# An attention and feed-forward block on one NeuronCore: three projection jobs of the second batch moved in halves behind the first row maxima

## The chip, the cores and the metric

The kernel runs on 1 core of one Trainium2 chip. The metric is the device time in microseconds (us) of one execution; lower is better. The kernel before took 443.47 us, the median of 3 runs (442.30 to 444.01).

## What is computed

Two batches of 1024 tokens with 128 features pass through 16-head attention (8 features a head), a residual with a layer norm, a feed-forward part of gated and GELU layers with 512 hidden features, and a second residual with a layer norm. Cut to what matters here:

```python
q, k, v = proj(wq, bq), proj(wk, bk), proj(wv, bv)   # x @ w.T + b, split into 16 heads
scores = einsum('bhqd,bhkd->bhqk', q, k) / sqrt(16)
out = einsum('bhqk,bhkd->bhqd', softmax(scores, axis=-1), v)
x = layernorm(x + out @ wo.T + bo)
x = layernorm(x + ffn(x))
```

The softmax takes the maximum of each row of scores before the exponential, so the kernel computes all scores twice: once for the maxima alone, and once, with the keys on the partitions, for the exponential.

## The kernel before, in words

**Work units.** The attention is cut into 16 units, each of 4 heads and 512 query rows of one batch. For each unit the maxima of its rows are found by 16 *turns*; a turn computes the scores of one head and 128 query rows against all 1024 keys (two matmuls of 512 columns), and the vector engine (DVE) reduces them to one maximum a row. The maxima of a unit are split into three bfloat16 parts by GpSimd (POOL, `split_max`), turned by TensorE (PE, `turn_max`), copied out of PSUM by ScalarE (ACT, `copy_max`) and written by two DMAs of the SyncE queue (SP, `load_max`, L466 and L406) into extra rows of the query tile `qx`, so that the second pass subtracts the maximum inside its matmul.

**The order of the work.** There is no scheduler: every engine has its own program written out in order, and waits on semaphores. PE's program at the start is: nine fill matmuls, the four projection jobs of the first batch (`job(0)` to `job(3)`, L1234), two matmuls that give the difference of the keys of the two halves (L1256, L1257), the v projection (L1263), then projection jobs of the second batch, then the first maxima. A projection job is one chunk of 512 tokens times the weights of q or k (`JOBS`, L188: of the second batch k of chunk 2, k of chunk 3, q of chunk 2, q of chunk 3, which are jobs 4 to 7). `AHEAD_JOBS` (L190) says how many of the eight jobs run whole before the first maxima; a later one runs as two `half_job`s of 256 columns (L1237), one behind each turn.

**The first maxima.** The first 27 turns (`WHOLE`) go without scores beside them. The first five (`FOLD`) are *unfolded*: two matmuls by `turn_half` (L1291) and one reduction over 1024 columns on DVE (`turn`, L958). Turns 5 to 26 are *folded*: `fold_apart` (L1319) computes the scores against the difference of the key halves, ACT copies its positive part out of PSUM (`copy_over`, L685), `fold_first` (L1307) computes the scores of the first half, and DVE adds both and reduces 512 columns instead of 1024 (`turn_folded`, L967). `busy` (L1223) issues fill matmuls whose result nobody reads. Turn 0 waits for the first rows of k and q, which SP and ACT load back from DRAM (`rows_first`, L1287), and for the four v chunks that DVE takes out of the same banks (`v_ready`, L1376).

**The evacuation of the jobs.** For each job of the second batch ACT copies the PSUM bank out with the bias (L655, which counts `proj_ready`), and makes the rounded copy (L658); POOL subtracts the two (L846), and SP stores the results to DRAM (L508, L512), where the units of the second batch load them. ACT's program has the four jobs (L653) ahead of its first `copy_over` (L687). PE waits for `proj_ready` to reach 4 (L1390) ahead of the first `fold_apart`.

**Behind it.** After turn 26 the main part begins: groups of three turn halves, three score matmuls (L1353, with `exp` on ACT, L664) and value products (L1369).

```python
JOBS = [("k", 0), ("k", 1), ("q", 0), ("q", 1), ("k", 2), ("k", 3), ("q", 2), ("q", 3)]
EARLY = 4
for t in range(FOLD):
    turn_half(2 * t)
    turn_half(2 * t + 1)
```

Of the kernel before, what the change touches and what calls it, by code (L numbers as in the profile page):

```python
# [42 lines left out]
C = 512  # L43
# [143 lines left out]

JOBS = [("k", 0), ("k", 1), ("q", 0), ("q", 1), ("k", 2), ("k", 3), ("q", 2), ("q", 3)]  # L188
EARLY = 4
WARM, OLD_FILL_BANK, FILL_BANK, AHEAD_JOBS = 9, 0, 7, 6  # L190


def gate_bank(c, m):
# [19 lines left out]
def build(nc, xT, wqT, wkT, wvT, woT, bq, bk, bv, bo, late,  # L213
          w1s, w2s, h1s, h2s, w3s, k_dram, q_dram, d_dram, den_dram, out):
    with ExitStack() as ctx:
# [3 lines left out]
        def sem(name):  # L219
            return ctx.enter_context(nc.semaphore(name))  # L220
# [43 lines left out]
        attn_c = xT_sb  # L264

        den_c = [sb(f"den_c{n}", [P, (u1 - u0) * C * HG // P]) for n, (_, u0, u1) in enumerate(MOVES)]
        v_sb = sb("v_sb", [P, G_ALL, KT, HG * DH])
        v_pad = sb("v_pad", [P, 2, KT, HG, 32])
# [45 lines left out]
        split_low = sem("split_low")  # L314
# [7 lines left out]
        proj_ready = sem("proj_ready")  # L322
# [896 lines left out]
        def _(pe):  # L1219
            def busy(n, bank, cols=C):  # L1220

                for _ in range(n):
                    nc.tensor.matmul(ps[:, bank, 0:cols], nonzero[:, 0, 0:P], nonzero[:, 0, 0:cols],  # L1223
                                     start=True, stop=True)
# [12 lines left out]
            def half_job(n, j):  # L1237

                name, c = JOBS[n]
                at = slice(j * C // 2, (j + 1) * C // 2)  # L1240
                ins = nc.tensor.matmul(ps[:, JOB_BANKS[n % 4], at], (wq_sb if name == "q" else wk_sb)[:],
                                       xT_sb[:, c * C + j * C // 2:c * C + (j + 1) * C // 2], start=True, stop=True)
                if j == 1:
                    ins.then_inc(job_done, 1)
# [25 lines left out]
            def turn_half(m):  # L1270

                t, part = m // 2, m % 2
                slot, qc, (h, q) = t // (QC * TURNS) % 2, t // TURNS % QC, head_of(t)
                at, h = slice(h // PAIR * GROUP, h // PAIR * GROUP + TROWS), h % PAIR
                if 2 * WHOLE <= m < 2 * WHOLE + 4:

                    pe.wait_ge(max_taken, 2 * (m - WHOLE - 3))
                elif m >= 4:

                    pe.wait_ge(max_taken, m - 3)  # L1280
                if part == 1 and t % (QC * TURNS) == 0 and t >= PER * TURNS:

                    pe.wait_ge(rows_late[slot], t // (PER * TURNS) * LOAD_INC[1])
                if part == 0:
                    if t == 0:

                        pe.wait_ge(rows_first, LOAD_INC[0])  # L1287
                    elif t % TURNS == 0:

                        pe.wait_ge(rows_in[slot][qc], (t // (PER * TURNS) + 1) * LOAD_INC[qc])  # L1290
                nc.tensor.matmul(ps[:, half_bank(m), :],  # L1291
                                       qx[at, slot, qc, h, q * P:(q + 1) * P],
                                       kx[at, slot, h, part * C:(part + 1) * C], start=True, stop=True)\
                  .then_inc(max_scores, 1)
# [84 lines left out]
            for t in range(FOLD):  # L1379
                turn_half(2 * t)  # L1380
                turn_half(2 * t + 1)
                if t < 2 * (len(JOBS) - AHEAD_JOBS):
                    half_job(AHEAD_JOBS + t // 2, t % 2)
                else:
                    pe.wait_ge(proj_ready, 1)
                    busy(1, OLD_FILL_BANK)
                    busy(1, OLD_FILL_BANK, C // 2)
            pe.wait_ge(kd_set, 2)
            pe.wait_ge(kd_in, LOAD_INC[1])
            pe.wait_ge(proj_ready, EARLY)  # L1390
# [259 lines left out]
```

## Time and profile before

| | |
|---|---|
| time, median of 3 runs | 443.47 us (442.30 to 444.01) |
| profiled execution, first to last instruction (span) | 441.5 us |
| that execution's own time | not listed beside the runs; the median lies 1.97 us above its span |
| PE busy | 427.8 us (97%) |
| DVE busy | 386.5 us (88%) |
| ACT busy | 367.7 us (83%) |
| POOL busy | 90.3 us (20%) |

A profile's row of a timeline has the start and the length in us, the engine, the line of the kernel, the operation, what it writes and reads, the number of instructions merged into the row, and in brackets how long the engine sat idle before it and what released it. `PEld` is PE's load of weights, `SPq` the queue of SyncE. A float32 matmul against the full weights stands as two instructions in the trace. Some matmul records are missing from a trace.

### The profile page before, as it was taken

The page shows a single profiled execution, that of the slowest core. Times are in us where ns is not written, and L with a number is a line of the kernel's source. Part 1 is how long each engine was busy: PE and PEld are TensorE (multiplying, and loading weights), DVE is VectorE, ACT ScalarE, POOL GpSimd, SP SyncE. Part 2 cuts the span into 40 slices and gives each one's busy share as a digit, 9 for nine tenths or more (in the row PEclk, how much of TensorE's full clock was granted, in tenths as well). Part 3 has the DMA queues.
Part 4 walks back from the last instruction along what each step waited for, and adds up shares of the span by engine and source line. Part 5 has one row for each costly group of instructions (what it writes and reads, how often), then busy time and mean ns, then how long its engine had stood idle before and what let it go on. Part 6 is the DMA issues. An engine that isn't in the chain of part 4 may idle for free.

```text
span 441.5 us, 9824 instructions
## 1 busy us (share of the span) xinstructions
PE 427.8 (97%) x3496; PEld 227.0 (51%) x3498; DVE 386.5 (88%) x719; ACT 367.7 (83%) x694; POOL 90.3 (20%) x142
## 2 busy tenths in 40 slices
PE   8999999999999999999999999999899899999995
PEld 4543544444444444444444443544333488877884
DVE  6799999999999999999999999999884577657636
ACT  4487989998998999989899899999899886678762
POOL 9730000100000010000001002373311263046103
PEclk9999999999999999999999999999999999999999
DMA  6567741111130110113011001021021000000101
GB/s 165 176 196 129 270 147 33 44 28 28 48 122 25 45 31 28 27 48 122 25 46 33 26 27 49 14 43 47 15 39 50 13 8 1 1 2 2 48 1 48
DMA packets 17117, 24.88 MB, mean 56 GB/s; under 512 B 5169, under 2 KB 9009, under 8 KB 16689
## 3 DMA queue, kind: packets, MB, share of 16 engines
q1 hardware_dynamic: 16464, 23.68, 19.3%
q10 hardware_dynamic: 608, 0.59, 0.5%
q8 instruction: 30, 0.49, 0.5%
q14 instruction: 15, 0.11, 0.1%
HBM read 15.08 MB, written 7.60 MB: 51 GB/s over the span
## 4 chain that ended last, share of the span: by engine, by line
PE 76%; DVE 10%; ACT 5%; SPq 3%; DMA 2%; issue 2%; POOL 0%; POOLq 0%; DVEq 0%; ACTq 0%
PE ps L1369 24%; PE ps L1291 20%; PE ps L1479 16%; DVE negmax L977 9%; PE ps L1353 8%; ACT arena L664 2%; DMA parts_q<-arena 2%; PE ps L1223 2%; PE ps L1234 1%; PE ps L1423 1%; PE ps L1319 1%; PE ps L1263 1%; SPq L463 1%; SPq L435 1%; ACT v_pad L722 1%
## 5 line engine op out<-in xcount | busy, mean ns | idle before, releaser
L977 DVE TENSOR_REDUCE negmax<-ps 128x1 f32<-128x512 f32 x458 | 275.8, 701 | 1.8 <-PE ps L1291 1.5
L664 ACT ACTIVATE arena<-ps 128x512 f32<-128x512 f32 x360 | 190.0, 606 | 19.3 <-PE ps L1353 14.1
L1353 PE MATMUL ps<-qx,kx 64*128 64x512 f32 x512 | 171.3, 451 | 0.9 <-DMA qx<-mT 0.6
L1291 PE MATMUL ps<-kx,qx 61*128 61x512 f32 x468 | 160.2, 441 | 0.6 <-DMA qx<-parts_q 0.5
L1291 PEld LDWEIGHTS ps<-kx,qx 61*128 61x128 f32 x468 | 75.1, 184 | 88.6 <-DVE negmax L977 79.3
L1369 PE MATMUL ps<-arena,v_pad 128*32 128x256 f32 (+3 forms) x1328 | 104.8, 407 | 2.8 <-ACT arena L664 2.8
L664 ACT ACTIVATE hf<-ps 128x512 f32<-128x512 f32 x152 | 83.2, 604 | 9.4 <-PE ps L1353 8.4
L1353 PEld LDWEIGHTS ps<-qx,kx 64*128 64x128 f32 x512 | 78.9, 184 | 18.6 <-ACT arena L664 11.8
L1479 PE MATMUL ps<-hid,w_high 128*128 128x512 f32 (+1 forms) x296 | 68.3, 388 | 0.8 <-issue 0.4
L1479 PEld LDWEIGHTS ps<-hid,w_high 128*128 128x128 f32 x296 | 54.2, 188 | 12.3 <-issue 0.8
L1369 PEld LDWEIGHTS ps<-arena,v_pad 128*32 128x32 f32 x1328 | 28.5, 108 | 37.1 <-issue 30.7
L1369 PE MATMUL ps<-hf,v_pad 128*32 128x128 f32 (+1 forms) x600 | 47.5, 388 | 0.0
L1120 DVE TENSOR_TENSOR hid<-hf,hid 128x512 fp32r<-128x512 f32 x32 | 23.0, 727 | 19.6 <-ACT hid L738 19.6
L829 POOL TENSOR_TENSOR mpart<-negmin,zeros 128x16 bf16<-128x16 f32 x15 | 3.3, 220 | 145.5 <-DVE negmin L987 145.5
L888 POOL TENSOR_TENSOR hid<-hf,hid 128x512 fp32r<-128x512 f32 x16 | 20.6, 1317 | 32.6 <-ACT hid L728 32.6
L1369 PEld LDWEIGHTS ps<-hf,v_pad 128*32 128x32 f32 x600 | 15.7, 109 | 16.1 <-issue 9.9
L809 POOL COPY v_pad<-v_sb 128x256 f32 (+1 forms) x8 | 3.1, 398 | 87.2 <-PE ps L1369 87.1
L737 ACT ACTIVATE hf<-ps,h2s_sb 128x512 f32<-128x512 f32 x16 | 11.0, 688 | 10.7 <-PE ps L1479 10.7
L737 ACT ACTIVATE hf<-ps,h1s_sb 128x512 f32<-128x512 f32 x16 | 11.0, 686 | 8.7 <-PE ps L1479 8.7
L1102 DVE SCALAR_TENSOR_TENSOR hf<-ps,w2s_sb,v_pad 128x512 f32<-128x512 f32 x16 | 11.5, 740 | 7.3 <-ACT v_pad L722 7.3
L857 POOL TENSOR_TENSOR w_low<-late_sb,w_high 128x512 fp32r<-128x512 f32 x11 | 14.1, 1282 | 16.4 <-ACT w_high L711 16.4
L1479 PE MATMUL ps<-prt,w_high 128*128 128x512 f32 x64 | 16.4, 403 | 0.6 <-DVE hf L1102 0.6
(107 smaller groups left out, 317.2 us busy)
## 6 DMA issues: line engine op xcount, KB each, us to landing
qx<-parts_q SPq DMA_DIRECT2D x60, 64.0 KB, 2.1
late_sb<-in_late SPq DMA_DIRECT2D x3, 1280.0 KB, 5.5
kx<-parts_k SPq DMA_DIRECT2D x56, 64.0 KB, 2.2
parts_q<-prt SPq DMA_DIRECT2D x3, 512.0 KB, 6.4
parts_q<-arena SPq DMA_DIRECT2D x3, 512.0 KB, 8.3
xT_sb<-in_xT SPq DMA_DIRECT2D x4, 256.0 KB, 4.2
xT_sb<-arena SPq DMA_DIRECT2D x28, 32.0 KB
prt<-den SPq DMA_DIRECT2D x7, 128.0 KB
```

The lines of the kernel that those rows point to most:

```text
L664: nc.scalar.activation(probs(n // HG)[:, heads(n), :], ps[:, PLAN["score", n][0], :], ACT.Exp, scale=SCALE).then_inc(exp_done, 1)
L737: nc.scalar.activation(hf[:, m % RING, :], bank, ACT.Gelu, scale=scale).then_inc(gelu_done, 1)
L857: nc.gpsimd.tensor_tensor(half(w_low[:, n, :]), w_sb[:, n, :], w_high[:, n, :], ALU.subtract).then_inc(w_left, 1)
L888: nc.gpsimd.tensor_tensor(half(dst[:, 1, m, :]), hf[:, m % RING, :], dst[:, 0, m, :], ALU.subtract).then_inc(gate_ready, 1)
L977: nc.vector.tensor_reduce(negmax[:, t // TURNS % 2, m % 2, h * QT + q:h * QT + q + 1], ps[:, MAX_BANK + m % 4, :], AX.X, ALU.max, negate=T ...
L1102: return nc.vector.scalar_tensor_tensor(out=out, in0=ps[:, gate_bank(c, m) + 1, :], scalar=s_sb["w2s"][:, m:m + 1], in1=gate[:, m % 2, :], ...
L1120: nc.vector.tensor_tensor(half(dst[:, 1, m, :]), hf[:, m % RING, :], dst[:, 0, m, :], ALU.subtract).then_inc(gelu_ready, 1)
L1223: nc.tensor.matmul(ps[:, bank, 0:cols], nonzero[:, 0, 0:P], nonzero[:, 0, 0:cols], start=True, stop=True)
L1291: nc.tensor.matmul(ps[:, half_bank(m), :], qx[at, slot, qc, h, q * P:(q + 1) * P], kx[at, slot, h, part * C:(part + 1) * C], start=True, s ...
L1353: nc.tensor.matmul(ps[:, bank, :], kx[at, slot, h % PAIR, kt * P:(kt + 1) * P], qx[at, slot, qc, h % PAIR, :], start=True, stop=True)\
L1369: ins = nc.tensor.matmul(ps[32 * n:32 * n + 32, PLAN["pv", w][0], c0:c1], v_pad[:, w // QC % 2, kt, n, :], probs(k)[:, n, c0:c1], start=(k ...
L1479: return nc.tensor.matmul(dsts[n], half(stationary), half(moving), start=start, stop=stop)
```

## The change

`AHEAD_JOBS` goes from 6 to 5. Job 5 (k of chunk 3) no longer runs whole ahead of turn 0. Jobs 5, 6 and 7 run as six halves: one behind each of the five unfolded turns, and the sixth, the second half of job 7, directly behind the fifth. The wait for `proj_ready` and the two fill matmuls behind turn 4 go away, and `half_job` gains the wait for the bank (`split_low`) that `job` has.

```diff
-WARM, OLD_FILL_BANK, FILL_BANK, AHEAD_JOBS = 9, 0, 7, 6
+WARM, FILL_BANK, AHEAD_JOBS = 9, 7, 5
...
             def half_job(n, j):
 
                 name, c = JOBS[n]
+                if j == 0:
+                    pe.wait_ge(split_low, n - EARLY + 1)
...
             for t in range(FOLD):
                 turn_half(2 * t)
                 turn_half(2 * t + 1)
-                if t < 2 * (len(JOBS) - AHEAD_JOBS):
-                    half_job(AHEAD_JOBS + t // 2, t % 2)
-                else:
-                    pe.wait_ge(proj_ready, 1)
-                    busy(1, OLD_FILL_BANK)
-                    busy(1, OLD_FILL_BANK, C // 2)
+                half_job(AHEAD_JOBS + t // 2, t % 2)
+            half_job(len(JOBS) - 1, 1)
             pe.wait_ge(kd_set, 2)
             pe.wait_ge(kd_in, LOAD_INC[1])
             pe.wait_ge(proj_ready, EARLY)
```

The lines below L1237 move down by two or up by two; ACT, DVE and SP have the same instructions in the same order, and POOL too. PE's order changes at two places. At the first, between the v projection and turn 1, PE has before (L1234 a whole job, L1291 the two halves of a turn, L1241 a half job):

```order
L1263 MATMUL ps<-wv_sb,xT_sb 128x128 x16
L1234 MATMUL ps<-xT_sb,wk_sb 128x512 x2
L1291 MATMUL ps<-kx,qx 128x512 x2
L1241 MATMUL ps<-xT_sb,wq_sb 128x256
L1291 MATMUL ps<-kx,qx 128x512 x2
```

and now (L1265, L1293 and L1243 are the same lines, shifted):

```order
L1265 MATMUL ps<-wv_sb,xT_sb 128x128 x16
L1234 MATMUL ps<-xT_sb,wk_sb 128x512
L1293 MATMUL ps<-kx,qx 128x512 x2
L1243 MATMUL ps<-xT_sb,wk_sb 128x256
L1293 MATMUL ps<-kx,qx 128x512 x2
```

One whole job less stands ahead of turn 0, and the half behind turn 0 is now one of the moved k job. At the second place, from turn 3 to the first folded pair (L1319, L1307), PE has before:

```order
L1291 MATMUL ps<-kx,qx 128x512 x2
L1241 MATMUL ps<-xT_sb,wq_sb 128x256
L1291 MATMUL ps<-kx,qx 128x512 x2
L1223 MATMUL ps<-hf 128x512
L1223 MATMUL ps<-hf 128x256
L1319 MATMUL ps<-w_high,qx 128x512 x2
L1307 MATMUL ps<-kx,qx 128x512 x2
```

and now:

```order
L1293 MATMUL ps<-kx,qx 128x512 x2
L1243 MATMUL ps<-xT_sb,wq_sb 128x256
L1293 MATMUL ps<-kx,qx 128x512 x2
L1243 MATMUL ps<-xT_sb,wq_sb 128x256 x2
L1321 MATMUL ps<-w_high,qx 128x512 x2
L1309 MATMUL ps<-kx,qx 128x512 x2
```

The two fills behind turn 4 have given way to the two halves of job 7, of which the last stood ahead of turn 4 before.

## Rows read from the trace of the kernel before

**Rows 1.** The page: span, busy time of each engine, granted clock by slice.
```profile
span 441.5 us, 9824 instructions
...
PE 427.8 (97%) x3496; PEld 227.0 (51%) x3498; DVE 386.5 (88%) x719; ACT 367.7 (83%) x694; POOL 90.3 (20%) x142
...
PEclk9999999999999999999999999999999999999999
```

**Rows 2.** Chain that ended last, in order: start us, us, what.
```profile
13.84 1.72 PE ps L1234 x4
15.56 0.66 PE ps L1291 x2
16.22 0.63 PE ps L1241 x2
...
20.76 0.70 ACT late_sb L655
...
32.90 0.29 ACT mT L672
33.21 0.92 SPq L406
```

**Rows 3.** Windows: span; PE, PEld, DVE, ACT, POOL busy; PEclk; DMA share; GB/s.
```profile
56.40:200.00 143.60, 142.82 (x1444) 66.46 (x1446) 143.00 (x246) 129.19 (x254) 8.44 (x36) 1.00 0.16 49
```

**Rows 4.** Timeline of PE, 15 to 28 us.
```profile
15.49 0.73 PE L1291 MATMUL ps<-kx,qx 61*128 61x512 f32 x2
...
20.02 0.70 PE L1241 MATMUL ps<-xT_sb,wq_sb 128*128 128x256 f32 x2
20.65 0.73 PE L1291 MATMUL ps<-kx,qx 61*128 61x512 f32 x2
21.54 0.27 PE L1223 MATMUL ps<-hf 128*128 128x256 bf16 x1 [0.16 <-ACT late_sb L655]
21.74 0.50 PE L1319 MATMUL ps<-w_high,qx 61*128 61x512 f32 x2
...
27.68 0.85 PE L1319 MATMUL ps<-w_high,qx 61*128 61x512 f32 x2
```

**Rows 5.** Timeline of ACT, 20 to 33 us.
```profile
20.76 0.69 ACT L655 ACTIVATE late_sb<-ps,bq_sb 128x512 f32<-128x512 f32 x1 [1.23 <-PE ps L1241]
21.48 0.63 ACT L658 ACTIVATE prt<-late_sb 128x512 fp32r<-128x512 f32 x1
22.28 2.18 ACT L685 ACTIVATE arena<-ps 128x512 f32<-128x512 f32 x4 [0.17 <-PE ps L1319]
...
29.66 3.35 ACT L685 ACTIVATE arena<-ps 128x512 f32<-128x512 f32 x6 [0.37 <-PE ps L1319]
```

**Rows 6.** Timeline of DVE, 13 to 37 us.
```profile
13.88 0.69 DVE L946 TENSOR_TENSOR v_sb<-ps,bv_bc 128x512 f32<-128x512 f32 x1 [0.20 <-PE ps L1263]
...
16.33 6.37 DVE L958 TENSOR_REDUCE negmax<-ps 128x1 f32<-128x1024 f32 x5 [1.72 <-PE ps L1291]
23.01 0.69 DVE L967 CUSTOM_DVE_ANT_0 arena<-ps,arena 128x512 f32<-128x512 f32 x1 [0.30 <-ACT arena L685]
...
36.65 0.69 DVE L977 TENSOR_REDUCE negmax<-ps 128x1 f32<-128x512 f32 x1
```

**Rows 7.** SP's last two loads for turn 0: lengths in ns, starts, landing.
```profile
L400 SPq DMA_DIRECT2D qx<-parts_q x2: 418/419/420, 12.2 to 12.6; - x2
...
DMA to landing us min/median/max: 2.1/2.2/2.2
```

**Rows 8.** Timeline of ACT, the last four copies of the folded turns.
```profile
33.19 2.27 ACT L685 ACTIVATE arena<-ps 128x512 f32<-128x512 f32 x4
```

**Rows 9.** Timeline of PE, the fills that wait for these copies.
```profile
35.60 0.59 PE L1223 MATMUL ps<-hf 128*128 128x512 bf16 x2 [0.48 <-ACT arena L685]
```

**Rows 10.** Timeline of POOL, the first step of splitting unit 0's maxima.
```profile
29.97 0.22 POOL L829 TENSOR_TENSOR mpart<-negmax,zeros 128x16 bf16<-128x16 f32 x1 [4.65 <-DVE negmax L967]
```

**Rows 11.** SP's waits, 14 to 60 us: total us, times, longest.
```profile
SPq L406 <- ACT mT L672: 3.4, 1, 3.4
```

**Rows 12.** Timeline of PE at the wait for unit 1's maxima.
```profile
56.37 0.47 PE L1353 MATMUL ps<-qx,kx 64*128 64x512 f32 x1 [0.58 <-DMA qx<-mT]
```

**Rows 13.** PE's waits, whole span: total us, times, longest.
```profile
PE ps L1369 <- ACT arena L664: 2.8, 5, 0.9
```

## The prediction, made before the changed kernel was run

> **What bounds the kernel now.** I read four views, from the whole to the place of the change. The page [rows 1] comes first: PE is busy for 97% of the span, DVE for 88%, ACT for 83%, and the clock row stands at 9 tenths or more in all slices, so no time is lost to TensorE's lower clock. Shares over the whole span do not say what a start-up change is worth; two other views do. The chain that ended last [rows 2] runs in the start-up through PE without a gap (two whole jobs, then turn, half job, turn, half job), at 20.76 through ACT's evacuation of job 7, later through ACT's copy of the first maxima at 32.90 and at 33.21 into SP's queue. The windows [rows 3] show what follows: from 56.4 to 200 us DVE is busy for 143.0 of 143.6 us and PE for 142.8. There is nothing there to catch up with, so whatever moves the instant at which the main part starts should move the end by about as much.
>
> The timelines then show who waits for whom at the change. On PE [rows 4] turn 0 begins at 15.49 the moment the whole jobs let go, the second half of job 7 runs from 20.02 to 20.72, turn 4 follows, and the first folded pair starts at 21.74. On ACT [rows 5] the evacuation of job 7 begins at 20.76, its rounded copy ends at 22.11 (21.48 + 0.63), and the first copy of a folded turn begins at 22.28, released by PE. On DVE [rows 6] the five unfolded turns go from 16.33 to 22.70, DVE waits 0.30 us for ACT's first copy, starts the first folded turn at 23.01 and then has 22 of them without a gap worth naming until 36.65, 0.62 us each. So the start of the folded turns on DVE is set by ACT, and ACT stands behind the last projection job.
>
> **The change, part by part.**
>
> *Turn 0 earlier.* One whole job (half of 1.72 us, 0.86 [rows 2]) leaves the place ahead of turn 0. Job 4 now ends at 13.84 + 0.86 = 14.70. Turn 0 has two other conditions. DVE's fourth v chunk ends at 14.57 (13.88 + 0.69 [rows 6]). Its rows are loaded by SP: the last issue starts at 12.6 and lands 2.1 to 2.2 us later [rows 7], so at 14.7 to 14.8. From the release to a matmul I take 0.14 us: ACT's last folded copy ends at 33.19 + 2.27 = 35.46 [rows 8], and PE's fills that wait for it start at 35.60 [rows 9]. Turn 0 then starts at 14.94 instead of 15.49, 0.55 us earlier: not the whole 0.86, since the load is late next.
>
> *Six half jobs for four.* A turn takes PE 0.66 us and a half job 0.63 [rows 2]. Split in halves, job 5 costs 1.26 us instead of 0.86, with a weight load exposed at each half. From turn 0 to the end of job 7 PE now has 5 turns and 6 halves, 3.30 + 3.78 = 7.08 us. The last two halves stand side by side with the same weights; in the whole jobs a matmul record of 512 columns takes 1.72 / 4 = 0.43 us, so a half with hidden weights would take 0.43 in two records, and the last half may be up to 0.20 cheaper. I take 6.98. Job 7 ends at 14.94 + 6.98 = 21.92, against 20.72 before: **1.20 us later**, though everything started 0.55 earlier. It ended ahead of turn 4 before; now turn 4 and one half more stand before it.
>
> *What waits for job 7.* ACT starts its evacuation 0.04 us after the end (20.72 to 20.76), at 21.96; it takes 0.69, to 22.65. PE needs it for `proj_ready` at 4, so the first folded pair starts at 22.65 + 0.14 = 22.79 against 21.74, 1.05 later. ACT's own order gives the same: evacuation and rounded copy take 1.35 us (20.76 to 22.11), to 23.31, and the first folded copy needs PE's pair, which came 0.54 us ahead of it before (21.74 to 22.28), so it starts at 23.33 against 22.28. DVE's first folded turn then moves from 23.01 to 24.06, **1.05 us later**, though DVE is through with the unfolded ones about 0.55 us earlier: it waits for ACT for some 1.9 us instead of 0.30.
>
> *The fills and the waits.* The two fills behind turn 4 lie in a time in which PE waits for ACT now anyway: nothing. The added waits for `split_low` ask for splits that DVE has done before the v chunk of 13.88 [rows 6], since DVE works in order: nothing. POOL gets job 7's copies 1.2 us later, but sat idle for 4.65 us ahead of the maxima at 29.97 [rows 10]: hidden. SP stores the results of these jobs behind the maxima in its own order, which is later still: hidden.
>
> *What may give some back.* At turn 16 the pair on PE took 0.85 us instead of 0.50 (27.68 against 21.74 [rows 4]), because the query rows of unit 1 had just landed, and ACT lost 0.37 us behind it [rows 5]. The load does not move, so this wait vanishes once the turns come a microsecond later. DVE had no gap there, so on DVE's side nothing is gained; if ACT's copies are what decides, the delay shrinks by 0.37.
>
> *To the end.* DVE's folded turns, the copy of the maxima at 32.90 and SP's write at 33.21 [rows 2] follow one after the other. SP had waited 3.4 us for that copy [rows 11], so its queue moves by the same amount, and it is SP's queue that PE waits for again at 56.37 [rows 12]. From there DVE and PE are full [rows 3].
>
> The sum is +1.05 us on the profiled span, 441.5 to 442.5. That execution's own time is not listed; the median of the runs, 443.47, lies 1.97 above its span, and I carry that over: **444.5 us**. The bounds of the terms are +0.58 (the last half as cheap as it can be, which is 0.10 less, and the 0.37 given back) and +1.15 (no saving on the last half). I stay near the upper end because DVE, not ACT, goes without a gap through the folded turns.
>
> **A rule against this change.** The change leaves PE idle for about 0.9 us between job 7 and the first folded pair, where fills stood. The trace has a wait of that length elsewhere, 0.9 us of PE on ACT [rows 13], and the clock row shows no slice below 9 tenths [rows 1]. The Trainium skill (TensorE: Matmul & The Clock Gate, section "A second HAM failure mode: psum-queue depth-cycling") says that short idle stretches between groups of matmuls, when frequent, can let TensorE fall to its lower clock and back. By that rule the time would come out as in the third rival below; by the rows it costs nothing.
>
> **The rivals.**
>
> *The earlier start carries through.* If the folded turns could begin as soon as DVE is free, the 0.55 us of turn 0 would be the gain: 443.47 - 0.55 = 442.9 us. For it: turn 0 does start earlier, and DVE stood idle for 1.72 us ahead of it [rows 6]. Against it: ACT's copy, which DVE waited for already [rows 6], is behind job 7's evacuation in ACT's own order. It needs halves that cost PE far less than 0.63 us. Chance 0.12.
>
> *Swallowed.* The delay ends in waits that stood there before: the 0.37 on ACT [rows 5] and the 0.58 us at 56.37 [rows 12], for instance if SP's queue there were held by landings that do not move. Then 1.05 - 0.37 - 0.58 = 0.1, or 443.6 us. Against it: SP's wait of 3.4 us [rows 11] says that its queue starts with the maxima. Chance 0.13.
>
> *The clock falls: slower.* If PE's clock goes to the lower of its two levels (1.2 and 2.4 GHz) in the idle 0.9 us, a round of the fold loop, which now takes two of DVE's folded turns, 1.24 us, would be set by PE: its work in a round lies near 1.15 us (0.50 for the pair [rows 4], 0.59 for two fills [rows 9], something for `fold_first`), and doubled it is 2.3, about 1.1 us more a round. One round already makes +2.15 in all, three make 444.5 + 3.3 = 447.8 us, all eleven 456.6. It decides from the first round on. Chance 0.05.
>
> That the change does not do what it says is excluded by the order of the instructions.
>
> **How the numbers follow.** The forecast, 444.5 us with its own range 444.0 to 445.1, has 0.66; the rivals 0.12, 0.13 and 0.05; 0.04 is left for a slower time of another kind. The runs before spread from 442.30 to 444.01, so a median of a few runs can be off by half a microsecond. The range reaches down to the first rival and up to the upper bound with that scatter: 442.8 to 445.7. A measurement of this kernel tells about 0.5%, 2.2 us, from no change: the forecast, +0.2%, and the first two rivals lie within, so 0.88 for the same, 0.03 for faster (a quarter of the first rival, by scatter) and 0.09 for slower (the clock and the rest).
>
> **What would show it.** In the profile after, PE's turn 0 starts near 14.9, the last half job ends near 21.9, the first folded pair starts near 22.8 with about 0.9 us idle ahead of it released by ACT L655; ACT's first L685 row starts near 23.3, DVE's first folded row near 24.1, ACT's copy of the maxima near 33.9. The forecast is wrong if DVE's first folded turn comes before 23.0, if that delay is gone again by SP's L406, or if PE's clock row dips.

## The result and the profile after

The changed kernel takes **443.84 us**, the median of 20 runs (443.32 to 445.98), against 443.04 us for the kernel before in 20 runs of the same comparison (442.20 to 444.01). The ratio is 1.0023, with a 95% interval of 1.0015 to 1.0031: about 1.0 us slower (0.0023 x 443). The medians lie 0.80 us apart; three of the 20 executions of the changed kernel took over 445 us, and they weigh more in the ratio than in the median. The prediction had +1.05 us and 444.5 us.

The page of the kernel after, for [rows 1]: span, busy time, granted clock by slice.

```profile
span 442.9 us, 9825 instructions
...
PE 428.8 (97%) x3498; PEld 228.0 (51%) x3498; DVE 386.4 (87%) x719; ACT 368.4 (83%) x694; POOL 90.5 (20%) x142
...
PEclk9999999999999999999999999999999999999998
```

The engines have as much to do as before, and the clock row has no dip in the start-up. Its 8 stands in the last of 40 slices, at the end of the span. What differs has to be looked for in waits. The timeline of PE after, for [rows 4]:

```profile
14.53 1.02 PE L1234 MATMUL ps<-xT_sb,wk_sb 128*128 128x512 f32 x2
16.03 0.69 PE L1293 MATMUL ps<-kx,qx 61*128 61x512 f32 x2 [0.48 <-DMA qx<-parts_q]
...
21.81 1.13 PE L1243 MATMUL ps<-xT_sb,wq_sb 128*128 128x256 f32 x4
23.81 0.49 PE L1321 MATMUL ps<-w_high,qx 61*128 61x512 f32 x2 [0.87 <-ACT late_sb L655]
...
29.72 0.52 PE L1321 MATMUL ps<-w_high,qx 61*128 61x512 f32 x2
```

Turn 0 is now released by the landing of its rows, and no longer by the jobs. The two halves of job 7 stand side by side and end at 22.94 (21.81 + 1.13). PE then stands idle for 0.87 us until ACT's evacuation has counted `proj_ready`. The timelines of ACT and of DVE after, for [rows 5] and [rows 6]:

```profile
22.98 0.69 ACT L655 ACTIVATE late_sb<-ps,bq_sb 128x512 f32<-128x512 f32 x1 [0.37 <-PE ps L1243]
23.70 0.63 ACT L658 ACTIVATE prt<-late_sb 128x512 fp32r<-128x512 f32 x1
24.31 10.70 ACT L685 ACTIVATE arena<-ps 128x512 f32<-128x512 f32 x18
34.90 0.29 ACT L672 ACTIVATE mT<-ps 128x128 f32<-128x128 bf16 x1
```

```profile
16.84 6.38 DVE L958 TENSOR_REDUCE negmax<-ps 128x1 f32<-128x1024 f32 x5 [1.38 <-PE ps L1293]
25.05 0.69 DVE L967 CUSTOM_DVE_ANT_0 arena<-ps,arena 128x512 f32<-128x512 f32 x1 [1.84 <-ACT arena L685]
...
38.66 0.69 DVE L977 TENSOR_REDUCE negmax<-ps 128x1 f32<-128x512 f32 x1
```

ACT's first folded copy begins the moment the rounded copy of job 7 ends, and DVE, which waited 0.30 us for that copy before, waits 1.84.

The whole start-up of this profiled execution lies later than before, which is not the change's doing: its first fills and jobs, the same instructions in the same order as before, ran slower. Two rows of each timeline of PE, before and then after:

```profile
1.25 3.62 PE L1223 MATMUL ps<-hf 128*128 128x512 bf16 x9 [1.25 <-DVE hf L933]
...
4.86 1.98 PE L1234 MATMUL ps<-xT_sb,wk_sb 128*128 128x512 f32 x4
```

```profile
1.26 4.02 PE L1223 MATMUL ps<-hf 128*128 128x512 bf16 x9 [1.26 <-DVE hf L933]
...
5.07 2.62 PE L1234 MATMUL ps<-xT_sb,wk_sb 128*128 128x512 f32 x4
```

What slowed them no view says; the clock row shows nothing here in either profile. So I compare stretches. Job 4 is the first job of the second batch; its first matmul starts at 13.68 before and at 14.53 after. In the 13 profiles of this document it starts from 13.47 to 14.89 where job 5 stands whole ahead of turn 0, and from 13.89 to 14.53 where it does not, so this start varies from execution to execution. The stretch from there to DVE's first folded turn is called the lead-in below.

| stretch, us | before | after | difference |
|---|---|---|---|
| start to job 4's first matmul | 13.68 | 14.53 | +0.85 |
| job 4 to turn 0 | 1.81 | 1.50 | -0.31 |
| turn 0 to the end of job 7 | 5.23 | 6.91 | +1.68 |
| turn 0 to DVE's first folded turn | 7.52 | 9.02 | +1.50 |
| **lead-in: job 4 to DVE's first folded turn** | 9.33 | 10.52 | **+1.19** |
| first folded turn to the main part (DVE's first L977) | 13.64 | 13.61 | -0.03 |
| main part to the end of the span | 404.85 | 404.24 | -0.61 |

The lead-in took 1.19 us more, and all of it was still there where the main part starts. The -0.61 behind it is looked at last.

### The profile page after: what moved, and what is told of

Same layout as the page of the kernel before. It is cut to its first block, busy times and chain, and to the rows that moved or that the text cites. A ratio compares the mean times of both kernels' runs of the same rounds, so it can differ in the third digit from the quotient of the medians.

```text
span 442.9 us, 9825 instructions
## 1 busy us (share of the span) xinstructions
PE 428.8 (97%) x3498; PEld 228.0 (51%) x3498; DVE 386.4 (87%) x719; ACT 368.4 (83%) x694; POOL 90.5 (20%) x142
## 4 chain that ended last, share of the span: by engine, by line
PE 78%; DVE 11%; ACT 5%; issue 2%; DMA 1%; POOL 0%; SPq 0%; POOLq 0%; DVEq 0%; ACTq 0%
PE ps L1371 25%; PE ps L1293 21%; PE ps L1477 15%; DVE negmax L977 9%; PE ps L1355 9%; ACT arena L664 2%; PE ps L1223 2%; PE ps L1421 1%; PE ps L1321 1%; PE ps L1243 1%; PE ps L1309 1%; ACT v_pad L722 1%; DMA qx<-parts_q 1%; PE ps L1431 0%; DVE hf L1102 0%
## 5 line engine op out<-in xcount | busy, mean ns | idle before, releaser
L977 DVE TENSOR_REDUCE negmax<-ps 128x1 f32<-128x512 f32 x458 | 275.8, 724 | 1.2 <-PE ps L1293 0.9
L664 ACT ACTIVATE arena<-ps 128x512 f32<-128x512 f32 x360 | 190.3, 607 | 19.0 <-PE ps L1355 13.4
L1293 PE MATMUL ps<-kx,qx 61*128 61x512 f32 x468 | 160.0, 441 | 0.8 <-DMA qx<-parts_q 0.5
L1293 PEld LDWEIGHTS ps<-kx,qx 61*128 61x128 f32 x468 | 75.0, 184 | 88.4 <-DVE negmax L977 78.6
L664 ACT ACTIVATE hf<-ps 128x512 f32<-128x512 f32 x152 | 83.4, 605 | 8.6 <-PE ps L1355 7.2
```

The source lines that it names most:

```text
L664: nc.scalar.activation(probs(n // HG)[:, heads(n), :], ps[:, PLAN["score", n][0], :], ACT.Exp, scale=SCALE).then_inc(exp_done, 1)
L977: nc.vector.tensor_reduce(negmax[:, t // TURNS % 2, m % 2, h * QT + q:h * QT + q + 1], ps[:, MAX_BANK + m % 4, :], AX.X, ALU.max, negate=T ...
L1293: nc.tensor.matmul(ps[:, half_bank(m), :], qx[at, slot, qc, h, q * P:(q + 1) * P], kx[at, slot, h, part * C:(part + 1) * C], start=True, s ...
```

## The experiments

The theory: the time follows the lead-in, which is set by the end of the last moved job, through ACT's order and PE's wait for `proj_ready` alike. The rivals: one of the two waits alone decides; the removed fills matter; the time comes from elsewhere in the program. Each ratio is taken against executions of the kernel before that ran beside the kernel named; their medians lie between 442.94 and 443.37 us, so two rows are compared by their ratios and not by their medians. In all diffs the line numbers shift by a few.

| kernel | job 4 to turn 0, us | turn 0 to first folded turn, us | lead-in | median of runs, us | ratio to before (95%) |
|---|---|---|---|---|---|
| before | 1.81 | 7.52 | 9.33 | 443.04 | 1 |
| the change | 1.50 | 9.02 | 10.52 | 443.84 | 1.0023 (1.0015 to 1.0031) |
| e3_job7_ahead | 1.26 | 8.54 | 9.80 | 443.38 | 1.0006 (0.9996 to 1.0017) |
| e5_pe_not_waiting | 1.37 | 8.93 | 10.30 | 443.83 | 1.0019 (1.0010 to 1.0028) |
| e7_act_alone | 1.18 | 9.02 | 10.20 | 443.90 | 1.0025 (1.0013 to 1.0036) |
| e6_both | 1.20 | 8.27 | 9.47 | 443.53 | 1.0012 (1.0002 to 1.0022) |
| e2_fills_back | 1.32 | 9.03 | 10.35 | 443.56 | 1.0014 (1.0002 to 1.0027) |
| e1_last_half_behind | 1.81 | 8.46 | 10.27 | 443.23 | 1.0015 (0.9998 to 1.0032) |
| e10_last_half_again | 1.81 | 8.16 | 9.97 | 444.84 | 1.0031 (1.0013 to 1.0049) |
| e8_last_half_and_fills | 1.81 | 8.16 | 9.97 | 444.23 | 1.0022 (1.0012 to 1.0032) |
| e11_fills_again | 1.81 | 8.16 | 9.97 | 443.44 | 1.0008 (0.9996 to 1.0020) |
| e4_whole_job6 | 1.81 | 6.87 | 8.68 | 442.40 | 0.9991 (0.9978 to 1.0003) |
| e9_whole_job6_again | 1.82 | 6.87 | 8.69 | 442.61 | 0.9987 (0.9975 to 0.9998) |

The lead-in of `e1_last_half_behind` holds 0.30 us more than that of the same kernel in `e10_last_half_again`, because its profile was already under the lower clock at the first folded pair, as shown below.

### Job 7's end moved back ahead of the fifth turn

From the changed kernel, with both halves of job 7 behind turn 3:

```diff
-                half_job(AHEAD_JOBS + t // 2, t % 2)
-            half_job(len(JOBS) - 1, 1)
+                if t < FOLD - 1:
+                    half_job(AHEAD_JOBS + t // 2, t % 2)
+                if t == FOLD - 2:
+                    half_job(len(JOBS) - 1, 0)
+                    half_job(len(JOBS) - 1, 1)
```

> The changed kernel with both halves of job 7 moved ahead of turn 4, so that turn 4 covers their evacuation. Theory: job 7 ends about 0.6 us earlier against turn 0, D near 9.9, ratio to before about 1.001, 0.5 us below the changed kernel. Rival (the number of halves or the place of job 5 decides): D near 10.5, ratio 1.002.

The timeline of PE in this kernel:

```profile
15.39 0.70 PE L1293 MATMUL ps<-kx,qx 61*128 61x512 f32 x2 [0.23 <-DMA qx<-parts_q]
...
19.89 1.56 PE L1243 MATMUL ps<-xT_sb,wq_sb 128*128 128x256 f32 x6
21.38 0.73 PE L1293 MATMUL ps<-kx,qx 61*128 61x512 f32 x2
22.70 0.50 PE L1321 MATMUL ps<-w_high,qx 61*128 61x512 f32 x2 [0.59 <-ACT late_sb L655]
```

Three half jobs in a row take 1.56 us, and turn 4 now covers part of ACT's evacuation. Turn 0 to the first folded turn shrinks from 9.02 to 8.54, and the time with it, from +1.0 to +0.3 us (0.0006 x 443). The order of the halves alone, with the same work, moves the lead-in as the end of job 7 does. The time moves the same way, but its interval (-0.2 to +0.8 us) holds zero and overlaps that of the change.

### PE's wait, ACT's order, and both

`e5_pe_not_waiting` lets PE start the first folded pair after three evacuations, and asks for the fourth ahead of the first fill of the fold loop. In `e7_act_alone` PE waits as in the change, but ACT makes the rounded copy of job 7 only behind the first four folded copies. `e6_both` has both edits.

```diff
-            pe.wait_ge(proj_ready, EARLY)
+            pe.wait_ge(proj_ready, EARLY - 1)
             for t in range(FOLD, WHOLE, 2):
...
+                if t == FOLD:
+                    pe.wait_ge(proj_ready, EARLY)
                 busy(1, FILL_BANK)
```

```diff
                   .then_inc(proj_ready, 1)
-                act.wait_ge(proj_ready, n + 1)
...
+                if n < EARLY - 1:
+                    round_job(n)
...
                 copy_over(t)
+                if t == FOLD + 3:
+                    round_job(EARLY - 1)
```

> The changed kernel, but PE waits for three evacuated jobs ahead of the first folded pair (its banks are those of jobs 4 to 6) and for the fourth only ahead of the first fill, which writes job 7's bank. Let F be the time from turn 0's first matmul to DVE's first folded turn: 7.52 us before, 9.02 after. Theory: ACT's own order (evacuation and rounded copy of job 7 ahead of the first folded copy) holds the folded turns as well, so PE's pair comes 0.9 us earlier, F stays 8.9 to 9.0, and the time is that of the changed kernel (ratio 1.002). Rival (PE's wait alone holds them): F near 8.2, ratio 1.000 to 1.001.

> The changed kernel with the rounded copy of job 7 on ACT put behind the first four folded copies; PE waits as in the changed kernel. Theory: PE's pair now holds the folded turns alone, F stays near 9.0, and the copy costs DVE a gap of about 0.4 us at the fifth folded turn: time of the changed kernel or 0.3 us more (ratio 1.002 to 1.003). Rival (ACT's order alone holds them): F near 8.4, ratio 1.001.

> Both edits, the shorter wait on PE and the later rounded copy on ACT. Theory: only with both gone do the folded turns start sooner, F near 8.4 (job 7's evacuation of 0.7 us still stands ahead of them on ACT); some 0.4 of the 0.6 us is given back at the fifth folded turn, where ACT now makes the copy: ratio 1.001 to 1.002. Rival (neither holds them, the end of turn 4 does): F near 9.0.

The timeline of ACT without PE's wait, `e5_pe_not_waiting`:

```profile
22.21 0.69 ACT L655 ACTIVATE late_sb<-ps,bq_sb 128x512 f32<-128x512 f32 x1 [0.37 <-PE ps L1243]
22.93 0.63 ACT L658 ACTIVATE prt<-late_sb 128x512 fp32r<-128x512 f32 x1
23.47 2.04 ACT L685 ACTIVATE arena<-ps 128x512 f32<-128x512 f32 x4
```

PE's pair stands there at 22.10, ahead of ACT's evacuation, and still ACT's first folded copy comes behind the rounded copy: turn 0 to the first folded turn is 8.93, not shorter than 9.02 by anything that counts. The timeline of ACT with ACT's order alone changed, `e7_act_alone`:

```profile
22.20 0.69 ACT L662 ACTIVATE late_sb<-ps,bq_sb 128x512 f32<-128x512 f32 x1 [0.37 <-PE ps L1251]
23.53 2.22 ACT L691 ACTIVATE arena<-ps 128x512 f32<-128x512 f32 x4 [0.65 <-PE ps L1329]
25.63 0.63 ACT L657 ACTIVATE prt<-late_sb 128x512 fp32r<-128x512 f32 x1
```

Now ACT is free at 22.89 and waits 0.65 us for PE's pair: 9.02 again. Only with both edits does the copy follow the evacuation at once, in the timeline of ACT of `e6_both`:

```profile
22.49 0.69 ACT L662 ACTIVATE late_sb<-ps,bq_sb 128x512 f32<-128x512 f32 x1 [0.37 <-PE ps L1251]
23.07 2.21 ACT L691 ACTIVATE arena<-ps 128x512 f32<-128x512 f32 x4
```

The stretch falls to 8.27 and the time to +0.5 us. The lead-in of 9.47 is 0.14 above before, and the moved copy leaves DVE a gap of 0.17 us ahead of its fifth folded turn; together that is 0.3 us, within the interval (0.1 to 1.0 us). So each of the two waits is enough to hold the folded turns, and neither alone is the cause.

### The fills

To the changed kernel, behind the last half of job 7, the two fills come back (into bank 0):

```diff
             half_job(len(JOBS) - 1, 1)
+            pe.wait_ge(proj_ready, 1)
+            busy(1, 0)
+            busy(1, 0, C // 2)
```

> The changed kernel with the two fill matmuls put back, behind the last half of job 7. Theory: they run inside PE's idle 0.87 us, so D stays near 10.5 and the time is that of the changed kernel (ratio 1.002 to before). Rival (the missing fills cost): the time comes back towards before, ratio 1.000 to 1.001, with the granted clock changed in this stretch.

Turn 0 to the first folded turn stays at 9.03, and the interval of the time, +0.1 to +1.2 us around +0.6, overlaps that of the change. So in the changed order the fills add nothing to the lead-in, and taking them out did not cause the loss.

### The neighbouring order, with and without fills

From the kernel before, only the second half of job 7 goes behind turn 4, and the fills and their wait are left out:

```diff
-                if t < 2 * (len(JOBS) - AHEAD_JOBS):
+                if t < 3:
                     half_job(AHEAD_JOBS + t // 2, t % 2)
-                else:
-                    pe.wait_ge(proj_ready, 1)
-                    busy(1, OLD_FILL_BANK)
-                    busy(1, OLD_FILL_BANK, C // 2)
+            half_job(len(JOBS) - 1, 1)
```

> The kernel before with one part of the change alone: job 5 stays whole ahead of turn 0, and only the last half of job 7 goes behind turn 4 (the fills there go away). Let D be the time from the first matmul of job 4 to DVE's first folded turn: 9.33 us before, 10.52 after. Theory (the folded turns wait for ACT, which waits for the end of job 7): job 7 ends 0.59 later against turn 0, the first folded pair starts 0.44 later, D near 9.8, and the time lies about 0.4 us above before (ratio 1.001). Rival (splitting job 5 and starting turn 0 earlier is what costs): D stays 9.33, ratio 1.000. Rival (the removed fills let TensorE's clock fall): a granted clock below 1.00 behind turn 4, and more than 1 us.

The twelve executions fall into two groups, eight of 442.80 to 443.34 us and four of 445.18 to 446.08. The profile was taken of one of the four. Its windows (length; PE, PEld, DVE, ACT and POOL busy; granted clock; DMA share; GB/s):

```profile
14.00:22.30 8.30, 7.65 (x23) 3.12 (x21) 6.31 (x7) 4.36 (x7) 5.93 (x6) 1.00 0.56 182
22.30:29.10 6.80, 6.49 (x22) 2.43 (x22) 4.20 (x12) 4.05 (x8) 3.08 (x2) 0.50 0.54 167
29.10:39.80 10.70, 10.24 (x53) 4.65 (x50) 10.05 (x34) 8.86 (x17) 0.88 (x4) 1.00 0.36 114
```

The granted clock stood at 0.50 for 6.80 us, the lower of the two levels, and DVE is busy for 4.20 of them, where the kernel before has this in the same stretch:

```profile
22.30:29.10 6.80, 6.80 (x34) 3.04 (x32) 6.50 (x20) 6.30 (x12) 2.96 (x2) 1.00 0.50 153
```

The timeline of PE in the profile with the last half behind turn 4:

```profile
21.04 0.70 PE L1241 MATMUL ps<-xT_sb,wq_sb 128*128 128x256 f32 x2
22.61 0.79 PE L1319 MATMUL ps<-w_high,qx 61*128 61x512 f32 x2 [0.87 <-ACT late_sb L655]
...
24.52 0.80 PE L1319 MATMUL ps<-w_high,qx 61*128 61x512 f32 x2
```

PE had worked up to the end of that half, at 21.74 (21.04 + 0.70), and then waited 0.87 us for ACT. The lower level began at 22.30, inside this wait, by the windows above (of the 8.30 us of the first window 7.65 are busy, and the last 0.56 are the start of the wait). PE came out of it at the lower level: the pair takes 0.79 instead of 0.50, and pairs stand 1.91 us apart (22.61 to 24.52) instead of about 1.24. This is the mechanism of the clock rival, in another order than the one changed; a round costs 0.67 us more (1.91 - 1.24), where that rival had 1.1. Was it this wait? I ran the same kernel again, and beside it one that has the wait and the two fills behind the last half:

```diff
             half_job(len(JOBS) - 1, 1)
+            pe.wait_ge(proj_ready, 1)
+            busy(1, OLD_FILL_BANK)
+            busy(1, OLD_FILL_BANK, C // 2)
```

> The run with only job 7's last half behind turn 4 (8 executions at 442.8 to 443.4 us and 4 at 445.2 to 446.1, and a profile in which the granted clock fell to half at 22.3 us for 6.8 us), with the two fills that the change removed put back behind that half. If the idle stretch that the fills leave open lets the clock fall: no execution above 445 and a granted clock of 1.00 in the fold loop, D near 9.9. If the clock falls for another reason: again about a third of the executions near 445.5.

> The run with only job 7's last half behind turn 4 and no fills a second time, beside the same with the fills, on one chip. If the idle stretch without fills lets the granted clock fall in some executions: again two groups, some executions 2 us or more above the others, which the one with the fills has not. If the two groups came from elsewhere: one group near 443.5 us, as with the fills.

> The same with the two fills behind job 7's last half, a second time, on the same chip. If the fills keep the clock: one group, no execution more than 1.5 us above the median, ratio 1.001 to 1.002.

Without fills, eight of the twelve executions of the second run took 444.68 to 448.17 us, and their mean granted clock over the execution was 0.996 or less. A mean of 0.996 alone proves no such fall, since one of the four others, at 442.78 us, has it too. The profile is of the one at 448.17; the clock row of its page, and its timelines of PE and of DVE:

```profile
PEclk9959999999999999999999999999999999999998
```

```profile
23.62 0.50 PE L1319 MATMUL ps<-w_high,qx 61*128 61x512 f32 x2 [0.87 <-ACT late_sb L655]
...
25.04 0.80 PE L1319 MATMUL ps<-w_high,qx 61*128 61x512 f32 x2
```

```profile
28.50 0.69 DVE L967 CUSTOM_DVE_ANT_0 arena<-ps,arena 128x512 f32<-128x512 f32 x1 [0.59 <-ACT arena L685]
...
30.41 0.69 DVE L967 CUSTOM_DVE_ANT_0 arena<-ps,arena 128x512 f32<-128x512 f32 x1 [0.60 <-ACT arena L685]
...
32.31 0.69 DVE L967 CUSTOM_DVE_ANT_0 arena<-ps,arena 128x512 f32<-128x512 f32 x1 [0.60 <-ACT arena L685]
```

Here the pair behind the same wait of 0.87 us still ran at 0.50, and the lower level shows from the next pair on, 1.42 us later (25.04 - 23.62). So the fall comes in the wait or in the round behind it. While the clock is down, DVE loses some 0.6 us every second folded turn. With the fills, none of 24 executions had a mean clock below 0.997, and none took over 444.69 us. The timeline of PE of `e8_last_half_and_fills`:

```profile
22.38 0.49 PE L1223 MATMUL ps<-hf 128*128 128x512 bf16 x2
23.41 0.50 PE L1319 MATMUL ps<-w_high,qx 61*128 61x512 f32 x2 [0.55 <-ACT late_sb L655]
```

The fills shorten the wait from 0.87 to 0.55 us, the pair comes at the same distance from turn 0, and it runs at 0.50. So in this order the fills keep the clock up. The Trainium skill (TensorE: Matmul & The Clock Gate, section "A second HAM failure mode: psum-queue depth-cycling") says that short idle stretches of PE between groups of matmuls, when they are frequent, can send its clock down and back. These runs agree in part: the clock went down and came back, after 6.8 us in the first profile, but there is one such stretch here, of 0.87 us, and no run tests how often it has to come. Why the changed kernel, with the same 0.87 us of idle, shows no sign of such a fall in its 20 executions (mean clock 0.997 or more), nor `e7_act_alone` in its 10, is **not settled**. Two half jobs side by side (1.13 us) stand ahead of the wait there, and one (0.70 us) here, but no run separates that.

In this order job 5 stands whole ahead of turn 0 as before, and yet the lead-in is 0.64 us longer: the place of job 7's end moves the folded turns without any split of job 5. In the two comparisons the order with fills measured +1.0 and +0.35 us (0.0022 and 0.0008 x 443), so two comparisons of one kernel can differ by more than half a microsecond.

### Going the other way

If the time follows the lead-in, an order with an earlier end of job 7 should beat both kernels. From the kernel before, with job 6 whole behind turn 1, the halves of job 7 behind turns 2 and 3, and nothing behind turn 4:

```diff
-                if t < 2 * (len(JOBS) - AHEAD_JOBS):
-                    half_job(AHEAD_JOBS + t // 2, t % 2)
-                else:
-                    pe.wait_ge(proj_ready, 1)
-                    busy(1, OLD_FILL_BANK)
-                    busy(1, OLD_FILL_BANK, C // 2)
+                if t == 1:
+                    job(AHEAD_JOBS)
+                elif 2 <= t < 4:
+                    half_job(AHEAD_JOBS + 1, t % 2)
```

> The kernel before with job 7 ended earlier: turn 0, turn 1, job 6 whole, turn 2, half of job 7, turn 3, other half, turn 4, no fills. Theory: job 7 ends near 5.0 us behind turn 0's start (5.2 before), the halves cost one weight load less, DVE's five unfolded turns run without gaps and end 7.0 us behind turn 0's start, D near 8.9, and the time is about 0.4 us below before (ratio 0.999). Rival (later waits, on the store of the second batch, swallow it): D near 8.9 but ratio 1.000.

> The kernel with job 6 whole behind turn 1 a second time, because its first interval (0.9978 to 1.0003) does not settle whether it beats the kernel before. Theory: DVE's first folded turn 0.65 us earlier from job 4 on, as in its profile, so a ratio of 0.9985 and both measurements together below 1. Rival (later waits swallow the gain): ratio 1.000.

The timelines of PE and of DVE of `e4_whole_job6`:

```profile
15.65 0.74 PE L1291 MATMUL ps<-kx,qx 61*128 61x512 f32 x4
16.32 1.12 PE L1234 MATMUL ps<-xT_sb,wq_sb 128*128 128x512 f32 x2
...
21.29 0.49 PE L1319 MATMUL ps<-w_high,qx 61*128 61x512 f32 x2 [0.21 <-ACT late_sb L655]
```

```profile
16.49 5.92 DVE L958 TENSOR_REDUCE negmax<-ps 128x1 f32<-128x1024 f32 x5 [1.72 <-PE ps L1291]
22.52 0.69 DVE L967 CUSTOM_DVE_ANT_0 arena<-ps,arena 128x512 f32<-128x512 f32 x1
```

DVE goes from its unfolded turns straight into the folded ones; its wait of 0.30 us [rows 6] is gone, and the unfolded turns end earlier too. The lead-in is 0.65 us shorter than before, and the time 0.4 and 0.6 us (0.0009 and 0.0013 x 443). Of the two intervals one lies wholly under 1 (0.9975 to 0.9998), and both lie under that of the change (1.0015 to 1.0031). So this order is faster than the changed kernel, and by the second comparison, just clear of the noise, than the kernel before.

### What is behind the main part's start

In the profile of the change the stretch from the main part to the end was 0.61 us shorter than before. The waits of SP's queue before, and then after (total, times, longest):

```profile
SPq L522 <- DMA parts_q<-arena: 1.8, 1, 1.8
```

```profile
SPq L406 <- ACT mT L672: 4.9, 1, 4.9
...
SPq L522 <- DMA parts_q<-arena: 0.4, 1, 0.4
```

The wait for stores is 1.4 us shorter, and PE's wait of 0.58 us for unit 1's maxima [rows 12] is not there after. That looks like the rival in which the delay is swallowed. But the same kernel run twice, whole job 6, differs in this stretch as much: 403.69 us without any wait at L522, and 404.54 us with this row:

```profile
SPq L522 <- DMA parts_q<-arena: 1.2, 1, 1.2
```

In all 13 profiles the stretch lies between 403.7 and 404.9 us, with the kernel before at the upper end. So -0.61 is within what one kernel does from execution to execution, and it is not put down to the change. Against a delay that is swallowed whole stand the comparisons: the change's 1.0 us, and in all nine other comparisons of kernels whose profile has the clock up a ratio on the same side of 1 as the lead-in, though three of their intervals hold 1 (`e3_job7_ahead`, `e11_fills_again`, `e4_whole_job6`). A part may be swallowed. Of the eleven profiles with the clock up, PE waits for unit 1's maxima in five (before, `e6_both`, `e8_last_half_and_fills`, `e9_whole_job6_again`, `e11_fills_again`: 0.36 to 0.58 us), where SP waits 0.7 us or more at L522, and in the six others it does not. Five of these six have job 5 split, but the sixth is `e4_whole_job6`, whose main part starts earliest of all. Whether up to half a microsecond of the delay is taken up there is **not settled**.

## Why the prediction was right

**The size.** +1.05 us was predicted; +1.0 was measured by the ratio and +0.80 between the medians. As a difference both lie within the bounds of the terms, +0.58 to +1.15. The time itself came out 0.66 us under the 444.5 of the sum: 443.84 lies in the wide range, 442.8 to 445.7, but below the forecast's own 444.0 to 445.1. The sum stood on 443.47, the median of 3 runs, and 20 runs put the kernel before at 443.04. The wide range also holds the times of the first two rivals, 442.9 and 443.6, so that the time lies in it says little. What tells the forecast from the first rival is the lead-in, which grew and did not shrink. Against the second, "swallowed", stands the difference of 1.0 us where that rival had 0.1, with an interval from 0.7 to 1.4. That the difference came within 0.05 is partly luck, since single terms missed by more, as follows.

**Turn 0 earlier.** 0.55 us predicted, 0.31 in this profile. The step was right in kind: the landing of the rows took over, as PE's row of turn 0 shows. Its size varies. In the five other kernels with one whole job ahead, job 4 to turn 0 takes 1.18 to 1.37 us, 0.44 to 0.63 less than before. The term was a sum of single rows of one execution, of which each shifts by a few tenths.

**Six halves for four.** Turn 0 to the end of job 7 was 6.98 us in the sum, and 6.91 in the profile. At the spacing of the others the two halves side by side would take 1.33 us (0.63 + 0.70); they take 1.13, so the saving is 0.20, the most that the text allowed, where it took 0.10. The other way, the sum left out the 0.07 by which a last half outlasts its spacing.

**What waits for job 7.** Idle of about 0.9 us on PE, released by L655: 0.87. First folded copy right behind the rounded copy, first folded turn 1.05 us later: in kind as said, 1.19 by the lead-in of this profile. That both ways lead to the same instant was a claim of the working, and `e5_pe_not_waiting`, `e7_act_alone` and `e6_both` show it: either hold is enough, and only with both loosened does the turn come 0.75 us nearer to turn 0 (9.02 to 8.27).

**What may give some back.** The pair of turn 16 takes 0.52 us (29.72), no longer 0.85, ACT copies 18 turns without a gap, and DVE had no gap there before: first folded turn to main part took 13.61 us, against 13.64. The wait vanished and gave nothing, as said.

**To the end.** ACT's copy of the maxima moved from 32.90 to 34.90, of which 0.85 is the late start of this execution, and SP's wait for it grew from 3.4 to 4.9 us: as said. That PE waits for SP's queue again at the maxima of unit 1 was so before, and is not so in this profile. Whether this link passes on the whole delay is open, as told above.

**Fills and clock.** Nothing for the fills was right, by `e2_fills_back`, and the clock rival did not come about in the changed kernel: the clock row of the start-up shows no dip. But the ground given for it, that 0.9 us of idle by the rows costs nothing, was too wide. One order away the same idle brought the clock down in part of the executions, and cost 2.4 and 3.6 us in the two profiles: turn 0 to the main part took 24.12 and 25.38 us there, against 21.76 and 21.75 in the same order with fills. The chance of 0.05 stood on a row of the whole span, [rows 13], whose wait is for ACT's `exp` (L664) in the main part, where the work around the wait is other work.

**Left open.** Three of the changed kernel's 20 executions took 445.07 to 445.98 us with a mean clock of 0.997 to 0.999, where the two executions whose profiles show a fall have 0.991 and 0.986, and the others of that order over 444.6 us have 0.996 or less. `e2_fills_back` and `e7_act_alone` have one such execution each (445.34 and 445.36 us, mean clock 0.997), and no execution of the kernel before took over 444.55. No profile is of one of these, and their cause is open. And the time follows the lead-in in sign, but not to a tenth: `e6_both` with a lead-in of +0.14 measured +0.5, `e3_job7_ahead` with +0.47 measured +0.3.

## What to carry to other kernels

Work that is pushed behind a consumer so that the consumer starts earlier has its price at its *last* piece: find where that ends, and which in-order engine has to take it away before it may go on with what the next stage needs. If two engines hold the next stage, loosening one of them shows nothing; try both before dropping the idea. And an idle time that is free in one place of the program is no proof for another place: look at the granted clock of every execution, not only of the one that was profiled.

## What was not expected of the hardware

The four matmuls of turns 0 and 1, put side by side by whole job 6, take 0.74 us together, where the two of one turn take 0.73 alone. That is a part of the shorter lead-in there. The heads of the two turns lie in other rows of the array by the code, as do those of a folded pair, which takes 0.50 us in the kernel before [rows 4], but no run tests whether that is the reason. Side by side in the program is not enough: in `e1_last_half_behind` turns 3 and 4, again of two heads, take twice as long.

```profile
19.56 1.55 PE L1291 MATMUL ps<-kx,qx 61*128 61x512 f32 x4
```

There turn 4 starts at 20.39, behind DVE's third unfolded turn (L958), whose bank it needs by the code; turn 3 is through by then.

The granted clock can go to its lower level in, or in the round behind, a wait of 0.87 us that follows work without a gap worth naming, and it does so in part of the executions of one and the same kernel (four of twelve, and eight of twelve, by their times and mean clocks).
